# The third expert layer with fixed places per expert: plain loads, direct scatters, routing in two batches

## The reference, cut to what matters

```python
x2 = layernorm(x).reshape(1024, 512)
g_s, u_s = jnp.split(x2 @ shared_w_gate_up.T, 2, axis=-1)      # shared part, 512 wide
shared_out = silu(g_s) * u_s @ shared_w_down.T
logits = x2 @ gate_w.T                                         # 1024 x 16
probs = softmax(logits)
topk_vals, topk_idx = top_k(probs, 2)
topk_vals = topk_vals / topk_vals.sum(-1, keepdims=True)
gu = einsum('th,eih->eti', x2, w_gate_up)                      # per expert: 512 -> 2 x 128
act = silu(g) * u
out_e = einsum('eti,ehi->eth', act, w_down)                    # 128 -> 512
x = x + tanh(g_ffn[2]) * (moe_out + shared_out)                # moe_out: the two chosen, weighed
```

## Time and profile before

| | |
|---|---|
| median of 3 runs (lowest to highest) | 2766.07 us (2759.72 to 2771.96) |
| the profiled execution | 2759.98 us |
| its span, first to last instruction | 2758.2 us |
| busy share: PE, DVE, ACT, POOL | 91%, 65%, 46%, 46% |
| granted TensorE clock, mean | 0.961 |

### The profile page before, as it was taken

How to read it: one execution, slowest core, us unless ns; L and a number is a source line. 1 busy time by engine, 2 the same in 40 slices (tenths; PEclk the granted TensorE clock), 3 DMA queues, 4 the chain that set the end, 5 groups by cost and what they waited for, 6 DMA issues and landing times.

```text
span 2758.2 us, 42059 instructions
## 1 busy us (share of the span) xinstructions
PE 2496.8 (91%) x13734; PEld 2092.5 (76%) x13734; DVE 1798.3 (65%) x3361; ACT 1267.1 (46%) x3698; POOL 1258.7 (46%) x1406
## 2 busy tenths in 40 slices
PE   4899999998889999999888888878679999999978
PEld 3788888887678888888766776755468888888853
DVE  4777777767677777777756666542277777777652
ACT  2454544554245555555525444213245555555421
POOL 4545544554134444444416556144345444444343
PEclk7999999999999999999999999989889999999989
DMA  3111111111012232101100001149601111110044
GB/s 119 49 31 35 35 38 33 36 39 32 7 31 89 96 101 100 51 31 39 66 8 9 9 8 39 54 128 322 206 24 50 36 39 39 35 33 27 30 192 154
DMA packets 66539, 172.63 MB, mean 63 GB/s; under 512 B 10227, under 2 KB 10929, under 8 KB 63898
## 3 DMA queue, kind: packets, MB, share of 16 engines
q1 hardware_dynamic: 50080, 112.49, 12.5%
q0 software_dynamic: 13040, 54.58, 5.9%
q10 hardware_dynamic: 3210, 2.89, 0.3%
HBM read 153.65 MB, written 33.16 MB: 68 GB/s over the span
## 4 chain that ended last, share of the span: by engine, by line
PE 76%; DVE 8%; POOL 5%; issue 5%; DMA 3%; ACT 3%; ACTq 0%; SPq 0%; POOLq 0%; DVEq 0%
PE B_qkv L705 29%; PE B_out L705 19%; PE B_oT L776 4%; PE B_s L756 4%; PE B_qT L746 3%; PE B_pt L766 3%; PE B_oT L705 2%; PE B_s L757 1%; PE B_oT L843 1%; PE B_out L1020 1%; POOL ring_l L1939 1%; DMA sq<-rows_x,tables 1%; PE B_qT L937 1%; PE B_s L705 1%; DMA raw<-in_pieces 1%
## 5 line engine op out<-in xcount | busy, mean ns | idle before, releaser
L1203 ACT ACTIVATE W<-S,nmx 128x128 f32<-128x128 f32 x768 | 298.0, 395 | 45.3 <-DVE nmx L1465 41.9
L1947 POOL TENSOR_SCALAR rn<-ss 128x5 f32<-128x5 f32 x128 | 25.5, 199 | 628.9 <-DVE ss L1408 628.9
L1100 ACT ACTIVATE sq<-B_qkv 128x640 f32<-128x640 f32 x128 | 90.5, 707 | 421.3 <-PE B_qkv L705 421.3
L1968 POOL TENSOR_TENSOR S<-S,mask 128x512 f32<-128x512 f32 x192 | 250.3, 1304 | 19.9 <-ACT S L1041 18.8
L1483 DVE SCALAR_TENSOR_TENSOR X<-B_out,gates,X 128x512 f32<-128x512 f32 x200 | 150.2, 751 | 159.2 <-PE B_out L705 159.0
L2007 POOL TENSOR_TENSOR W<-W,rden 128x512 f32<-128x512 f32 x192 | 199.7, 1040 | 81.5 <-DVE rden L1470 81.5
L705 PE MATMUL B_out<-ring_h,oT_h 128*128 128x512 f32 x516 | 205.9, 399 | 20.9 <-DVE kT L1455 9.1
L705 PE MATMUL B_qkv<-ring_h,xnT_h 128*128 128x512 f32 x512 | 214.9, 420 | 1.4 <-DVE xnT_l L1321 1.4
L756 PE MATMUL B_s<-kT,qT_h 128*128 128x256 f32 x768 | 203.5, 342 | 9.5 <-DVE xnT_l L1321 8.5
L705 PE MATMUL B_out<-ring_l,oT_h 128*128 128x512 f32 x516 | 204.8, 397 | 0.0
L705 PE MATMUL B_out<-ring_h,oT_l 128*128 128x512 f32 x516 | 204.5, 396 | 0.0
(11 more groups left out here) (459 smaller groups left out, 7999.1 us busy)
## 6 DMA issues: line engine op xcount, KB each, us to landing
raw<-in_pieces SPq DMA_DIRECT2D x270, 256.0 KB, 2.6
slots_x<-in_zero SPq DMA_DIRECT2D x16, 1030.0 KB
w<-in_experts SPq DMA_DIRECT2D x8, 1024.0 KB, 11.1
slots_y<-S SPq DMA_DIRECT2D x31, 256.0 KB
X<-in_x ACTq DMA_DIRECT2D x8, 256.0 KB, 3.2
raw<-in_ctxT SPq DMA_DIRECT2D x8, 256.0 KB, 2.7
rows_x<-xn SPq DMA_DIRECT2D x8, 256.0 KB, 2.1
raw<-in_quant SPq DMA_DIRECT2D x4, 256.0 KB, 2.7
```

Of the source, the lines that this page charges most:

```text
L1203: t = act.activation(W[:, k, cols(r)], S[:, k, cols(r)], ACT.Exp, bias=nmx[:, k, r:r + 1], accum_out=den[:, k, r:r + 1])
L1968: pool.tensor_tensor(S3, S3, m.unsqueeze(1).to_broadcast([P, R, P]), ALU.add).then_inc(*masked.now((layer, u)))
```

## The change

Each of the 16 experts gets a fixed region of 1024 rows in `slots_x`, which grows to 16 x 1024 rows and serves both expert layers. A row's place there is 1024 times its expert plus its rank, so it needs no table of tiles. The rows of X, not yet normalised and with their mean, 1/deviation and number in three more columns, are scattered straight to their two places (16 indirect DMAs of 258 KB), and `rows_x`, `ids`, `load_ids2` and `turn_ids2` go. Tile t < 16 is expert t's first tile: its weights and rows come by plain loads from SP. The other 15 tiles are indirect from POOL as before. DVE normalises each fetched tile of rows (`apply2`). Routing is done in two batches, blocks 0 to 5 and blocks 6 and 7. The two best are chosen from the logits. The zeroing stores are 32, from iteration 16 on. The landing times of the planner differ by stage.

```diff
+BATCHES = ((0, 6), (6, NB))
-LANDING2 = 1.1
-            self.at(i + 1, 61, "keep_rows2", b)
-        self.at(first - 5, 2, "fill_dispatch2")
-        for part in range(5):
-            self.at(first + part // 2, 76 + part % 2, "choose2", part)
-        self.at(first + 2, 78, "rank2")
-        self.at(first + 2, 79, "table2")
-        self.at(first + 3, 70, "scatter2")
-        self.at(first + 5, 70, "load_ids2")
-        self.at(first + len(self.steps2) - 2, 80, "turn_ids2")
+        self.at(first - 12, 2, "fill_dispatch2")
+        self.at(first - 11, 61, "choose2", 0, 0)
+        self.at(first - 10, 61, "choose2", 0, 1)
+        self.at(first - 6, 26, "both2", 0)
+        self.at(first - 6, 27, "rank2", 0)
+        self.at(first - 6, 28, "slots2", 0)
+        for b in range(NB):
+            self.at(*((first - 6, 29) if b < 2 else (first - 3, 61) if b < 6 else (first, 74.6)), "scatter2", b)
+        self.at(first - 1, 73, "choose2", 1, 0)
...
+        self.at(first, 74.2, "rank2", 1)
+        self.at(first, 74.4, "slots2", 1)
+        self.at(first + 1, 76, "table2")
+        self.at(first + 2, 76, "weigh2")
+        for t in range(4):
+            self.at(first + 2 + t, 77, "load_weights2", t)
         first += len(self.steps2) - 1
+        self.landings += [(first - 7, 0.9), (first, 2.1), (first + TILES2 + 2, LANDING)]
         for t in range(TILES2):
-            self.at(first - 3 if t < 4 else first + t - 2, 10, "fetch_weights2", t)
-            self.at(first + max(0, t - 2), 11, "fetch_rows2", t)
+            how = "load" if t < E2 else "fetch"
+            if t > 3:
+                self.at(first + t - 2, 10, f"{how}_weights2", t)
+            self.at(first + max(0, t - 2), 11, f"{how}_rows2", t)
+            self.at(first + t, 12, "apply2", t)
...
-            for n in range(E3 * T // CLEAR):
-                self.at(self.first[1] + 8 + 2 * n, 47, "clear_slots", n)
+            for n in range(E2 * T // CLEAR):
+                self.at(16 + 2 * n, 47, "clear_slots", n)
...
             def turn2(t):
-                pe.wait_ge(*rows_in[t % 2].of((2, t)))
+                pe.wait_ge(*row_normed.of((2, t)))
...
-                    n = pe.transpose(B_pt[:, cols(c)], rows2[t % 2][:, cols(c)], ident[:, :])
+                    n = pe.transpose(B_pt[:, cols(c)], xn[:, t % 2, cols(c)], ident[:, :])
...
+            def both2_made(batch):
+                at = slice(*BATCHES[batch])
+                if batch == 0:
+                    dve.wait_ge(*pv2.of((PAIRS - 1, 1)))
...
+                    dve.tensor_copy(X[:, :, D + 2].bitcast(I32), tokens2).then_inc(*onehot_made.now("numbers"))
+                    dve.tensor_copy(share2, share2_f)
+                    dve.tensor_copy(mid[:, 2 * P:4 * P], qk[:, 0:2 * P]).then_inc(*onehot_made.now("consts2"))
+                then()
+                dve.tensor_tensor(both2[:, at, :], first2[:, at, :], second2[:, at, :], ALU.add
+                                  ).then_inc(*onehot_made.now(("both2", batch)))
...
+            def apply2(t):
+                row = rows2[t % 2]
+                dve.wait_ge(*rows2_in(t))
...
+                dve.tensor_scalar(xn[:, t % 2, :], row[:, 0:D], row[:, D:D + 1], row[:, D + 1:D + 2], ALU.subtract, ALU.mult
+                                  ).then_inc(*row_normed.now((2, t)))
...
                     dve.wait_ge(*down_done.of((n, j)))
+                    if e == 0:
+                        dve.wait_ge(*rope_in[b].of(("slots", TOP2 - 1)))
...
+            def scatter2(b):
+                batch = [high > b for _, high in BATCHES].index(True)
+                pool.wait_ge(*slot_made.of(("ffn2", batch)))
...
+                pool.wait_ge(*rstd_done.of(("ffn2", b)))
                 for k in range(TOP2):
...
+                    pool.indirect_dma_start(out=slots_x, in_=X[:, b, :], in_offset=None,
+                                            out_offset=bass.IndirectOffsetOnAxis(ap=slot2_i[:, k, b:b + 1], axis=0)
+                                            ).then_inc(*rope_in[b].now(("slots", k)))
...
-                if t > 1:
-                    pool.wait_ge(*rows_turned.of((2, t - 2)))
...
+                pool.wait_ge(*row_normed.of((2, t - 2)))
...
+            def load_weights2(t):
+                if t == 0:
+                    sync.wait_ge(*pv2.of((PAIRS - 1, 1)))
+                if t > 3:
+                    sync.wait_ge(*tile_done.of((2, t - 4)))
+                sync.dma_start(raw2[:, t % 4, :], io["experts2"][cols(t), :]).then_inc(*x_in[t % 4].now(("w2", t)))
+
+            def load_rows2(t):
+
+                if t == 0:
+                    sync.wait_ge(*tabled.of("y_rows2"))
+                    for b in range(NB):
+                        sync.wait_ge(*rope_in[b].of(("slots", TOP2 - 1)))
+                if t > 1:
+                    sync.wait_ge(*row_normed.of((2, t - 2)))
+                sync.dma_start(rows2[t % 2], slots_x[t * T:t * T + P, :]).then_inc(*x_in[4 + t % 2].now(("rows2", t)))
```

More of the change, by code:

```diff
@@ L163, in small_heads @@
         self.five[2] = self.five[2] + self.need(range(base + 3, base + 5), first + 15, 0)
+        self.landings += [(first, 1.1)]
         self.at(first - 6, 90, "fill_tables")
@@ L341, in split_next @@
         item = self.landing[0]
-        first = self.first.get(2, now)
-        landing = LANDING2 if now is not None and first < now < first + CHUNKS else LANDING
-        if now is not None and item["when"] is not None and now - item["when"] < landing:
-            return
+        if now is not None and item["when"] is not None:
+            if now - item["when"] < max(((i, landing) for i, landing in self.landings if i <= now))[1]:
+                return
         if item["kind"] in ("float", "quantised") and item["half"] == 0:
@@ L903, in route2 @@
                 read["kT"] = route_exp.of(("ffn2", b))
-            def rank2():
-                pe.wait_ge(*onehot_made.of("both2"))
-                bank_free("sc")
-                places = both2.rearrange("p b e -> p (b e)")
-                pe.matmul(B_sc[:, 0:P], before, places, start=True, stop=False)
-                for n in range(1, NB):
-                    pe.matmul(B_sc[:, n * E2:P], ones, places[:, 0:P - n * E2], start=False, stop=False)
-                for b in range(NB):
-                    t = pe.matmul(B_sc[:, P:P + E2], ones, both2[:, b, :], start=False, stop=b == NB - 1)
-                t.then_inc(*ranked.now("ffn2"))
-                read["sc"] = tabled.of("place2")
@@ L1243, in route2, with weigh2 @@
                 copy(logits2[:, b, :], B_kT[:, 0:E2]).then_inc(*route_exp.now(("ffn2", b)))
-            def choose2(part):
-                if part == 1:
-                    act.wait_ge(*route_max.of("ffn2"))
-                    act.activation(prob2, temp2, ACT.Exp).then_inc(*route_exp.now("ffn2"))
+            def weigh2():
+                act.wait_ge(*route_max.of("ffn2"))
+                act.activation(per_row2[3], per_row2[2], ACT.Exp).then_inc(*route_exp.now("ffn2"))
             def turn2(t):
@@ L1608, in ffn1, with choose2, first_most @@
                 add_to_x(b, B_oT, gates[:, 5:6], ("ffn1", b))
-            def choose2(part):
-                gate = gates[:, 6:7]
-                best, total, inverse, most, place, top, other = (per_row2[k] for k in range(7))
-                weight = per_row2[7:9]
+            def choose2(batch, part):
+                at = slice(*BATCHES[batch])
+                n = at.stop - at.start
+                place, top, other = (m[:, at] for m in per_row2[4:7])
                 def per_expert(ap):
-                    return ap.unsqueeze(2).to_broadcast([P, NB, E2])
-                order = rev[:, 0:E2].unsqueeze(1).to_broadcast([P, NB, E2])
-                def first_most(onehot, src, value):
+                    return ap.unsqueeze(2).to_broadcast([P, n, E2])
+                order = rev[:, 0:E2].unsqueeze(1).to_broadcast([P, n, E2])
+                temp = temp2[:, at, :]
+                def first_most(onehot, values, value):
@@ L2186, in sync_program @@
                     parts[name](*args)
-            for done in (*landed, scales_in, cols_in, cleared, ids_in, *consts2_in, *rows_kept, dispatch_in, *y_stored, *scattered, *rows_in, *weight_in, *x_in, *small.values(), *rope_in):
+            for done in (*landed, scales_in, cols_in, cleared, *consts2_in, dispatch_in, *y_stored, *scattered, *rows_in, *weight_in, *x_in, *small.values(), *rope_in):
                 if done.made:
```

320 lines of the change are left out of this document (177 added, 143 removed).

## The result

| | before | after |
|---|---|---|
| median of 20 runs each, same chip | 2766.28 us | 2755.91 us |
| lowest to highest | 2756.52 to 2774.52 | 2745.75 to 2763.65 |
| ratio, 95% interval | | 0.9964 (0.9952 to 0.9975) |
| profiled execution, span | 2759.98, 2758.2 us | 2760.93, 2759.1 us |

10.4 us were saved, by the interval 7 to 13. Twelve more runs of after, beside another set of runs of before, gave 0.9974 (0.9964 to 0.9984). The forecast was 14.9.

The account below looks back on a forecast made before the run. PE was taken as full in attention, held up by POOL's serial DMA chain before the third expert layer's tiles, and with ACT bounding the tiles. -20.4 + 4.5 + 1 = -14.9 from 2766.07 gave 2751 us, range 2741 to 2767.

Parts of the forecast that it names:

- Part 1: From 1758 to the third expert layer's first tile: 8.5 instead of 28.9 us beyond the shared steps' work, -20.4 us.
- no chain through POOL's DMAs between the shared steps: Sign in the changed profile: shared up and down steps follow at 8.2 us, without POOL's DMAs between them.
- Part 2: New work before 1758: choice of six blocks, small tensors, first ranking, wait for scatters; +4.5 us, bounds 2 and 9.
- the four tensors: Behind the last product with v, PE waits until DVE has made four small tensors: 1.0 us.
- Part 3: The 31 tiles: -1 us for the first 16, +2 for the other 15 from normalising and hand-over; +1 us.
- Part 4: The rest of the kernel: 16 more 1 MB stores, all of them earlier, cost nothing; 0 us.
- A: Rival: pieces land earlier, the clock stays high from 1758, scatter waits vanish; -23 us, 2743 us, chance 0.13.
- B: Rival: DVE does not get through choice, table and sums beside the steps; -4 us, 2762 us, chance 0.14.
- C: Rival: SP's one queue makes tile rows late; decides from a 4.96 us period, 2775 us at 5.5, chance 0.10.
- D: Rival: 15 normalisings on DVE each hold POOL 0.55 us through the locked port; 2758 us, chance 0.04.
- wrong if the first turn is later than 1833: Sign of failure: the first tile's turn, expected at about 1825 to 1827, comes after 1833.
- The sign for the plain tiles: Sign of failure: the first 16 tiles, loaded plainly, have a period above 4.3 us; 4.03 was expected.

Follow-up runs that it names:

- rows_early: The changed kernel with the first two tiles' rows asked for and normalised one step earlier; 2754.18 us, ratio to before 0.9970.
- scatters_late: The changed kernel with POOL's scatters of the first six blocks issued behind the last shared splits; 2758.72 us, ratio to before 0.9990.
- weights_later: The changed kernel with weights asked for one tile later, so those ahead of the rows no longer wait for a tile's end; 2742.01 us, ratio to before 0.9919.
- best_split: The changed kernel with rows ahead of weights and the first ranking's products behind the first shared up step; 2746.58 us, ratio to before 0.9938.
- best_all: The edits of best_split and rows_early together on the changed kernel; 2740.61 us, ratio to before 0.9917.
- no_apply: The changed kernel without the normalising of each tile's rows, which are turned as they came; 2749.40 us, ratio to before 0.9955.
- after_again: The changed kernel run once more without edit, for a second profile; 2759.02 us, ratio to before 0.9974.
- rows_first: The changed kernel with each tile's rows asked for ahead of the weights of the tile after next; 2747.71 us, ratio to before 0.9938.

## Why the forecast was nearly right

By the medians the saving was 10.4 us instead of 14.9; by the stages of two profiles it was 9.4 and 8.0. Part 1 gave 1 to 2 us more than its forecast, which hid a part of what parts 2 and 3 cost beyond theirs, 7 to 9 us together.

**Part 1, -20.4: right, -21.8 and -22.4** (the second profile of after set against the second of before, here and below). What remained beyond the steps and their slow start, 61.5 - 52.2 - 2.2 = 7.1 us (8.5 by the forecast), is 1.9 for the second ranking (its last 15 products in the chain: 0.11 us each, not 0.215; the forecast had 3.7), 3.6 for the first turn (3.3), and 1.6 of slow products and short waits (1.5), of which 0.8 is that up(2) at its low clock took 3.0 us too long and not 2.2. `table2` lay beside the steps as assumed: no wait of PE for it. rows_early shows that the 3.3 were two costs that cover each other. scatters_late shows by the reverse edit that POOL's DMAs at this place do hold the steps; that the full 20 us come from the old chain is read from the two traces, not from an experiment that puts it back. The sign "no chain through POOL's DMAs between the shared steps" held only from up(2) on.

**Part 2, +4.5: too small, +7.7 and +6.7.** The wait for the four tensors is 2.0 us, not 1.0: DVE itself came to them only behind a split that it did at 1743.14, when the last product with v was over. The first ranking took 1.5 us, not 1.1, and what is left ahead of the gap, put down to the choice of six blocks, was 1.5 and 1.1 us (forecast 1.1). And I had priced no lower clock here, though my own rows showed one for the neighbouring step. Windows from the first up step's start to the second's, kernel after, first and second profile:

```profile
1745.95:1757.78 11.83, 10.90 (x37) 8.42 (x38) 3.70 (x7) 2.07 (x4) 4.11 (x5) 0.79 0.25 89
```

```profile
1743.72:1754.39 10.67, 9.73 (x37) 7.58 (x38) 3.71 (x7) 2.07 (x4) 4.11 (x5) 0.88 0.29 99
```

Before, the same distance was 9.4 us at a clock of 1.00 and 10.3 at 0.91. The eight profiles with the 2.0 us gap show 10.7 to 12.0 us, the two in which the ranking stands behind the step, best_split and best_all, 10.5 at 0.97. The scatter wait of 1.3 was 0.99 and reached PE (a wait of 3.66 us instead of 2.6 for block 7's rows).

**Part 3, +1: the step that failed, +4.7 and +7.6.** A mechanism was in the text: one round from a tile's end to the end of the tile four later is stretched by 0.85, or 0.21 a tile. 30 periods at 0.21 are 6.4 us, between the two measured. That agreement is in part luck: without the normalising the tiles still took 2.3 us more than before, and with the wait gone and the normalising kept they took 3.5 less. I charged the 0.85 for 15 tiles only, and took 1 us off for the other 16 because POOL's issues leave their path. They do, but SP's queue has the same form: rows behind weights, weights behind the end of a tile, and the landing is 6 to 7 us long whoever issues. I had also taken the loop's period from one tile, 4.03 us, and called it bound by PE and ACT; over 30 periods before took 4.15, so its rows were late already. The first 15 periods cost +1.6 and the last 15 +4.5 us on the mean of the two profiles, where the forecast had -1 and +2. weights_later shows that the wait at the head of the queue is what cost, and no_apply that the normalising was a part of it.

**Part 4, 0: right.** 850 to 1130 is full, and from 200 to 820, where the early zeroing stores are, PE's busy time is 588.0 of 620 us, 587.8 before.

**The rivals.** A did not occur: the waits in part 2 stayed, and between 1772 and 1789 the granted clock was 0.81 and 0.95. B was right in kind for part 2 alone, at 2 to 3 us. (Its sum has a slip: 6 and 5 us in place of 3.3 and 1.5 add 6.2, not 7.5. Nothing rests on it.) C named the right place, SP's one queue with the rows behind 768 KB and a wait, but a point from which it decides of 4.96 us a tile; the mean periods reached 4.31 and 4.40, 0.3 and 0.4 of that way from 4.03. D is not seen as a price: in after_again the indirect fetches of rows took 945 to 959 ns and those of weights 941 to 1169, median 945, with a normalising in every period (before, without it: 937 to 944); in rows_first the latter have a median of 1027. That is 0.1 to 0.2 us in single DMAs, and the loop ran at 4.0 us a tile with it. The Trainium skill's page SBUF — State Buffer, "SBUF: two separate sides", tells of the lock for VectorE operations in a two-port mode. Whether this normalising runs in such a mode no run here shows.

My sign "wrong if the first turn is later than 1833" was badly put: the turn came at 1833.70 in one profile, past the mark, and at 1830.31 in the other, with 6.5 and 4.7 us of it from upstream. A distance between two events of the same stage would have been the test. The sign for the plain tiles, a period above 4.3 us, was reached but not passed: 4.27 and 4.30 over the first 15 periods, where 4.03 was forecast.

## What to carry to other kernels

In an in-order DMA queue the wait of the front item is part of the lead of everything behind it: put the transfer whose place is free early ahead of one that waits for a late event, or let the latter be the one whose event is long past. When an operation is added between a landing and its use, ask what it frees as well as what it delays: it may be a buffer stage that pays only once the transfers are asked for earlier. Charge a per-round delay to every round that has it.

## What the runs showed of the hardware

- The same instructions of the fourth layer take 63.2 us at a granted clock of 0.97, 67.6 at 0.90 and 69.7 at 0.85, and 6 us lie between two profiles of one kernel. A stage far from a change that differs by this much says nothing of the change.
- The landing of 264 KB of rows is 6 to 7 us (5.4, 6.3, 7.6 minimum, median, maximum on POOL's queue in the kernel after) beside a load of 768 KB a tile at 273 to 297 GB/s, against 2.6 us for a piece at 89 GB/s. An earlier issue hardly shortens it (in rows_first 5.4, 6.3, 7.7 on POOL's queue, and a median of 6.9 instead of 7.3 on SP's); it moves it off the path.
- A gap of 2.0 us on PE was followed by a granted clock of 0.79 over the next 11.8 us in one profile and of 0.88 over the next 10.7 in another, in the same program at the same step. Compared in one fixed window (1745 to 1758) they read 0.77 and 0.95, because the step had moved by 2.2 us: windows have to move with the step.
